# A transformer megakernel on one core: head rows taken in turns from the partitions, a second chunk laid later, MLP weights loaded later

## The chip, the cores and the metric

One core of one Trainium2 chip runs the whole program. The metric is the device time of one execution in microseconds. The kernel before was run three times: 809.21 us is the median, 804.66 the lowest, 817.38 the highest. The execution that was profiled took 811.46 us; its span, from the first to the last instruction on the chip, is 809.7 us.

## What is computed

The input is a (4, 16, 16, 192) image batch, 1,024 tokens of 192 channels, all float32. Three transformer layers follow one another, then a small spectral layer. Each transformer layer is

```
y = layernorm(x);  q, k, v = y @ Wqkv + b            # 12 heads
attn = softmax(q*scale @ k.T + rel_h + rel_w)        # relative positions, decomposed by row and column
x = x + (attn @ v) @ Wproj + b
x = x + gelu(layernorm(x) @ W1 + b1) @ W2 + b2       # 192 -> 768 -> 192
```

Layers 0 and 2 have heads of 16 channels and attend within windows of 14 x 14 tokens (the 16 x 16 image is padded, so there are inner windows, border windows and pad keys). Layer 1 has heads of 48 channels and attends within whole images of 256 tokens. The last part is a Fourier transform of each image, two block-diagonal complex products with a bias, a ReLU and a soft shrink, and the inverse transform.

## The kernel before

Everything stays in SBUF. Five engines run five instruction streams. All of them walk the same list of steps, `all_steps()`, and each engine issues only its own part of a step, so this list alone sets the order on every engine; semaphores (`Count`) connect them. SyncE (SP) issues all DMAs from one queue, in the order of the list, and where it waits, every DMA behind it waits too.

A **chunk** is 96 rows (`CK`) of q and of k: six heads of 16 channels in layers 0 and 2 (two chunks), two heads of 48 in layer 1 (six chunks). For a chunk, TensorE computes q and k (steps `q`, `k`) and the relative terms (`rh`, `rw`) into PSUM, ScalarE copies them out, and they are split into a rounded part and a rest (three planes `QHL`, `KHL`: high, high, low; two planes in layer 1). In layers 0 and 2 VectorE splits q (lines 975 to 991) and GpSimd splits k (lines 765 to 780); in layer 1 GpSimd does both. The buffers `QHL`, `KHL` and `REL` hold one chunk, so a chunk's split may only overwrite them when all heads of the chunk before have been read (`chunk_read`).

The step **`aug`** of a head (lines 641 to 676) gathers its rows by DMA into one slot of the ring `QA`/`KA` (6 slots in layers 0 and 2, 4 in layer 1): `QA<-QHL` (line 656), `KA<-KHL` (line 664), `QA<-REL` (line 674). `QHL` and `KHL` are read from `mine = slice(i * hd, (i + 1) * hd)`, adjacent partitions; `REL` is read from every sixth partition (every second in layer 1). A later head can be gathered only after the `scores` of the head that had its slot.

For each head, TensorE forms the products twice. **`max`**: queries on the partitions, VectorE takes the row maxima (line 1016), splits them (lines 1029, 1033), and **`maxT`** transposes them (line 1184), copies them (line 1040), and writes them by two small DMAs (`QA<-NR`, line 686) as one more row of the head's `QA` slot, "the max row" below. **`scores`**: keys on the partitions, now with the max row, and ScalarE takes the exponential out of PSUM into `PT` (line 880). `max` has two PSUM banks, `scores` three. **`pv`** multiplies by the values for two heads at a time, in five units.

When the heads of a group are done (four in layers 0 and 2, two in layer 1): **`copy_o`** (ScalarE), **`sums`** (`SUMS<-XNOS`), a reciprocal and **`inverse`** (`inverses<-SUMS`, into DRAM), **`divide`** (`OT<-inverses`, 512 KB broadcast back, then GpSimd multiplies, line 792). Then come `proj`, the layer norm and the MLP, whose weights `W1`, `W2` (576 KB each) are loaded at step `scores` 9.0 (head 9, unit 0), lines 687 to 692.

In `windowed_attention` (layers 0 and 2) the list starts with the first chunk and the gathers of heads 0 to 5, then the values. Then stand `q`, `k`, `rh`, `rw` of the second chunk mixed with `max` of heads 0, 1 and 2, and then the main loop: `scores(h, k)` beside `max(h + 3, k)` and two or three `pv` units per head.

Of the kernel before, what the change touches and what calls it, by code (L numbers as in the profile page):

```python
# [32 lines left out]
HEADS, HALF = 12, 6  # L33
# [21 lines left out]
class Layer:  # L55


    def __init__(self, index, head_dim, window, eps, gelu):
# [168 lines left out]
def first_chunk(L, heads):  # L227

    early = [("q", 0, 0)] if L.pads else [("q", 0, 0), ("k", 0, 0)]
    out = [(*unit, 4 + k) for k, unit in enumerate(early)]  # L230
    out.append(("turn", 0, 1, 2))
    out += [(*unit, k % 4) for k, unit in enumerate(u for u in chunk_units(0) if u not in early)]
    out += [("aug", h, 0, 0) for h in range(heads)]
    return out + [("v", t, 0, 4 + 2 * (t % 2)) for t in range(L.vtiles)]


def windowed_attention(L):

    out = first_chunk(L, L.ring)
    units = chunk_units(1)  # L240
# [7 lines left out]
    late = []  # L248
    for h in range(HEADS):
        beside = {k: [] for k in range(L.units)}  # L250
        if h + ahead - 1 < HEADS:
            beside[1].append(("maxT", h + ahead - 1, 0, 0))
        for k, step in late:
            beside[k].append(step)
        late = []
        if h >= 2:
            pair = h // 2 * 2 - 2
            values = [("pv", pair, k, 0) for k in range(L.pv_steps)]
            for k, step in zip((1, 3, 5), values[:3]) if h % 2 == 0 else zip((1, 3), values[3:]):
                beside[k].append(step)  # L260
            if h % 2 and (pair + 2) % L.per_group == 0:
                g = pair // L.per_group
                beside[4] += [("copy_o", g, 0, 0), ("sums", g, 0, 0)]
                late = [(3, ("inverse", g, 0, 0)), (5, ("divide", g, 0, 0))]
        for k in range(L.units):
            out.append(("scores", h, k, 0))
            if k == L.units - 1 and h + L.ring < HEADS:
                out.append(("aug", h + L.ring, 0, 0))
            if h + ahead < HEADS:
                out.append(("max", h + ahead, k, 0))  # L270
            out += beside[k]
    out += [step for _, step in late]
    g = L.groups - 1
    out += [("pv", HEADS - 2, k, 0) for k in range(L.pv_steps)]
    return out + [("copy_o", g, 0, 0), ("sums", g, 0, 0), ("inverse", g, 0, 0), ("divide", g, 0, 0)]


def whole_attention(L):
# [24 lines left out]
    for h in range(0, HEADS, 2):  # L303
# [24 lines left out]
        if (h + 2) % L.per_group == 0:  # L328
            g = h // L.per_group
            out.append(("copy_o", g, 0, 0))  # L330
            out.append(("sums", g, 0, 0))
            finished = [("inverse", g, 0, 0), ("divide", g, 0, 0)]
        else:
            finished = []
    out += finished
    assert not units and not waiting
# [43 lines left out]
def _build(nc, ctx, io, out):  # L380
# [128 lines left out]
    probs_done = count("probs_done", per(lambda L: HEADS * L.units))  # L509
    pv_done = count("pv_done", per(lambda L: HEADS // 2 * L.pv_steps))  # L510
    o_copied = count("o_copied", per(lambda L: 2 * L.groups))
# [86 lines left out]
    def _(sp):  # L598
# [40 lines left out]
        for L, step, h, u, bank in all_steps():  # L639
            n, m = L.index, mem[L.index]  # L640
            if step == "aug":
# [4 lines left out]
                hd, end = L.hd, L.tiles - 1  # L646
                mine = slice(i * hd, (i + 1) * hd)

# [26 lines left out]
            elif step == "maxT":  # L675
# [63 lines left out]
    def _(pool):  # L739
# [23 lines left out]
        for L, step, i, u, bank in all_steps():  # L763
            n, m = L.index, mem[L.index]
            if step == "k" and u == 1 or step == "q" and u == 1 and not L.pads:

# [48 lines left out]
    def _(act):  # L815
        act.wait_ge(*first_in.at(0, 2))
        for L, step, i, u, bank in all_steps():
# [46 lines left out]
            elif step == "scores":  # L864
# [3 lines left out]
                if L.pads:  # L868
                    if h >= 4:
                        act.wait_ge(*pv_done.at(n, L.pv_steps * (h // 2 - 2) + min(k, 4)))  # L870
                    size, at, wide = ((HALF_IN, 2 * k * INNER, 2 * INNER) if k < 4 else
                                      (EDGES, 2 * FIRST_EDGE, 2 * EDGES) if k == 4 else
                                      (L.pc, 2 * FIRST_EDGE + 2 * EDGES, 4 * EDGES))
                    dst, src = m["PT"][0:size, h % 4, at:at + wide], PS[0:size, bank, 0:wide]
                else:
                    if h >= 2:
                        act.wait_ge(*pv_done.at(n, L.pv_steps * (h // 2 - 1) + 2 * (k // 2) + 1))
                    dst, src = m["PT"][:, h % 2, k % 2, (k // 2) * 512:(k // 2 + 1) * 512], PS[:, bank, :]
                act.wait_ge(*scores_psum.at(n, j))
# [37 lines left out]
    def _(dve):  # L917
# [9 lines left out]
        for L, step, i, u, bank in all_steps():  # L927
# [158 lines left out]
    def _(pe):  # L1086
# [12 lines left out]
        for L, step, i, u, bank in all_steps():  # L1099
# [117 lines left out]
            elif step == "pv":  # L1217

                pair = (i, i + 1)
                if i % L.per_group == 0 and u == 0:  # L1220
# [6 lines left out]
                if not L.pads:  # L1227
                    b = u
                    pe.wait_ge(*probs_done.at(n, L.units * (i + 1) + 2 * (u // 2) + 1))
                    for kc in range(2):  # L1230
# [5 lines left out]
                elif u < NB:  # L1236
                    b = u
                    pe.wait_ge(*probs_done.at(n, L.units * (i + 1) + u))
                    for kc in range(2):
# [6 lines left out]
                else:  # L1246
                    pe.wait_ge(*probs_done.at(n, L.units * (i + 1) + L.units - 1))
                    if i == 0:
# [82 lines left out]
def _pack(inputs):  # L1331
# [17 lines left out]
    for L, (prefix, keys) in zip(LAYERS, names):  # L1349
        n = L.index  # L1350
        g1, o1, g2, o2, rh, rw, wp, bp, w1, b1, w2, b2 = (f(prefix + k) for k in keys.split())
        if n == 1:
            wqkv = np.concatenate([f(prefix + k) for k in ("wq", "wk", "wv")], 1)
            bqkv = np.concatenate([f(prefix + k) for k in ("bq", "bk", "bv")])
        else:
            wqkv, bqkv = (f(prefix + k) for k in (("qkv_w", "qkv_b") if n == 0 else ("w_qkv", "b_qkv")))
        col = np.zeros((128, 8 + 2 * L.chunks + FM), np.float32)
        at = 0
# [43 lines left out]
```

## Time and profile before

| | |
|---|---|
| median of 3 runs | 809.21 us |
| profiled execution | 811.46 us, span 809.7 us |
| TensorE busy | 635.9 us (79%) |
| VectorE, ScalarE, GpSimd busy | 252.7, 224.5, 125.7 us |
| chain that ended last: TensorE, DMA, SP's queue | 49%, 17%, 14% |
| packets of SP's DMAs | 56.77 MB, 34.4% of 16 engines' span |

The times in a timeline are counted from the span's start. A number in square brackets behind a row is the engine's idle time just before it, and what ended it. "PEclk" is the TensorE clock that was granted, 1.00 being full (2.4 GHz) and 0.50 the lower level (1.2 GHz). Layer 0 lies at about 0 to 243 us, layer 1 at about 243 to 548, layer 2 at about 548 to 783.

### The profile page before, as it was taken

Reading aid. Unit: us, or ns where it says so; the run is one execution under the profiler, and the core shown is the slowest. Engines: PE = TensorE matmul, PEld = TensorE weight load, DVE = VectorE, ACT = ScalarE, POOL = GpSimd, SP = SyncE. Lnnn points to the kernel's source line nnn. Section 1 sums busy time; section 2 is a strip of 40 time slices with the busy share of each in tenths; the row PEclk is TensorE's granted clock in tenths of the full one; section 3 lists DMA queues with packets and bytes.
Section 4 is the critical chain, followed back from the end, with each engine's and each line's share of the span. In section 5 each row is a group of like instructions: output and inputs, shape, how many; then the busy total and the mean of one; then the engine's idle time right before and its main releaser. Section 6 shows DMA issues by size and latency. Waiting matters only on the chain.

```text
span 809.7 us, 9787 instructions
## 1 busy us (share of the span) xinstructions
PE 635.9 (79%) x3668; PEld 453.1 (56%) x3668; DVE 252.7 (31%) x727; ACT 224.5 (28%) x444; POOL 125.7 (16%) x189
## 2 busy tenths in 40 slices
PE   3916998784999999889696666998358987959997
PEld 1703775463666566557365455665227764636666
DVE  2405766004123424133142003124147760040023
ACT  2200445321332132323232211333004553213220
POOL 2301000112103303222230112203011001131011
PEclk9965699576999969999797688999766995669999
DMA  5790186212204266253527011302911853020001
GB/s 151 151 134 16 19 116 116 54 39 71 54 23 93 58 129 128 58 126 72 118 66 171 29 45 38 107 6 32 141 34 15 112 97 73 25 74 1 0 1 40
DMA packets 24601, 57.41 MB, mean 71 GB/s; under 512 B 7788, under 2 KB 12150, under 8 KB 24458
## 3 DMA queue, kind: packets, MB, share of 16 engines
q1 hardware_dynamic: 24554, 56.77, 34.4%
q8 instruction: 30, 0.49, 0.3%
q14 instruction: 17, 0.14, 0.0%
HBM read 16.93 MB, written 0.93 MB: 22 GB/s over the span
## 4 chain that ended last, share of the span: by engine, by line
PE 49%; DMA 17%; SPq 14%; DVE 8%; issue 6%; POOL 3%; ACT 2%; DVEq 0%; POOLq 0%; ACTq 0%
PE PS L1096 47%; DMA OT<-inverses 7%; SPq L656 4%; DVE NM L1016 3%; DMA QA<-REL 3%; SPq L674 3%; SPq L664 3%; DMA QA<-NR 3%; POOL OT L792 2%; DMA SUMS<-XNOS 2%; PE PS L1108 1%; SPq L686 1%; DMA inverses<-SUMS 1%; DMA PT<-in_qm 1%; SPq L618 1%
## 5 line engine op out<-in xcount | busy, mean ns | idle before, releaser
L1096 PE MATMUL PS<-KA,QA 104*98 104x196 f32 (+3 forms) x432 | 96.5, 326 | 70.1 <-DVE NM L1016 52.6
L1016 DVE TENSOR_REDUCE NM<-PS 98x2 f32<-98x392 f32 (+2 forms) x192 | 103.5, 569 | 84.4 <-PE PS L1096 83.3
L880 ACT ACTIVATE PT<-PS 98x392 f32<-98x392 f32 (+2 forms) x192 | 94.0, 516 | 111.0 <-PE PS L1096 108.7
L1096 PE MATMUL PS<-QA,KA 114*98 114x196 f32 (+2 forms) x480 | 104.6, 336 | 24.8 <-DMA QA<-NR 22.9
L1096 PEld LDWEIGHTS PS<-KA,QA 104*98 104x98 f32 (+3 forms) x432 | 67.1, 200 | 89.1 <-DVE NM L1016 58.3
L1096 PEld LDWEIGHTS PS<-QA,KA 114*98 114x98 f32 (+2 forms) x480 | 79.2, 220 | 51.7 <-DMA QA<-NR 24.6
L1096 PE MATMUL PS<-PT,V 98*32 98x196 f32 (+2 forms) x672 | 89.0, 394 | 1.3 <-ACT XNOS L895 1.3
L792 POOL TENSOR_TENSOR OT<-XNOS,OT 128x512 f32<-128x512 f32 x24 | 29.9, 1268 | 294.0 <-DMA OT<-inverses 294.0
L1096 PE MATMUL PS<-XT,WQKV 96*96 96x512 f32 x128 | 70.1, 687 | 4.7 <-issue 3.8
L1096 PE MATMUL PS<-XT,W 96*128 96x512 f32 x144 | 65.2, 607 | 3.4 <-issue 3.4
L1096 PE MATMUL PS<-WP,OT 128*128 128x192 f32 x192 | 41.1, 383 | 33.2 <-POOL OT L792 33.2
L1096 PEld LDWEIGHTS PS<-WP,OT 128*128 128x128 f32 x192 | 39.1, 230 | 34.8 <-POOL OT L792 27.0
L1096 PEld LDWEIGHTS PS<-PT,V 98*32 98x32 f32 (+2 forms) x672 | 40.4, 133 | 27.3 <-issue 5.2
L1096 PE MATMUL PS<-W,HT 128*128 128x192 f32 x288 | 48.7, 328 | 4.7 <-ACT HT L901 4.7
L1096 PEld LDWEIGHTS PS<-W,HT 128*128 128x128 f32 x288 | 46.6, 190 | 9.6 <-ACT HT L901 9.6
L1096 PEld LDWEIGHTS PS<-XT,W 96*128 96x128 f32 x144 | 27.4, 194 | 35.4 <-issue 34.6
L1003 DVE TENSOR_TENSOR REL<-PS,REL 32x512 fp32r<-32x512 f32 (+5 forms) x64 | 28.7, 479 | 55.6 <-ACT REL L862 55.6
L1046 DVE RECIPROCAL SUMS<-SUMS 128x32 f32<-128x32 f32 (+1 forms) x12 | 3.6, 303 | 129.9 <-DMA SUMS<-XNOS 129.9
L862 ACT ACTIVATE REL<-PS 32x512 fp32r<-32x512 f32 (+5 forms) x64 | 25.0, 429 | 64.2 <-PE PS L1096 62.3
L1096 PEld LDWEIGHTS PS<-XT,WQKV 96*96 96x96 f32 x128 | 22.7, 186 | 32.0 <-issue 31.8
L901 ACT ACTIVATE HT<-PS,COL 128x512 f32<-128x512 f32 x36 | 23.7, 687 | 49.4 <-PE PS L1096 49.4
L1096 PE MATMUL PS<-QD,RB 96*32 96x64 f32 x384 | 36.5, 262 | 0.1
(81 smaller groups left out, 617.9 us busy)
## 6 DMA issues: line engine op xcount, KB each, us to landing
QA<-QHL SPq DMA_DIRECT2D x36, 192.0 KB
OT<-inverses SPq DMA_DIRECT2D x12, 512.0 KB
KA<-KHL SPq DMA_DIRECT2D x24, 228.0 KB
QA<-REL SPq DMA_DIRECT2D x24, 224.0 KB
QA<-QHL SPq DMA_DIRECT2D x12, 384.0 KB
KA<-KHL SPq DMA_DIRECT2D x12, 384.0 KB
KA<-PT SPq DMA_DIRECT2D x12, 313.5 KB
W<-in_w SPq DMA_DIRECT2D x6, 576.0 KB, 7.5
```

The costliest lines, as they stand in the source:

```text
L618: sp.dma_start(raw(m["KA"][L.rel_row:L.rows, 0, s, :]), m["KC"]).then_inc(aug_const.sem, 16)
L656: sp.dma_start(raw(dst), raw(src)).then_inc(aug_in[s].sem, 16)
L664: sp.dma_start(raw(dst), raw(src)).then_inc(aug_in[s].sem, 16)
L674: sp.dma_start(raw(dst), raw(src)).then_inc(aug_in[s].sem, 16)
L686: sp.dma_start(raw(dst), raw(src)).then_inc(max_row_in[p].sem, 16)
L792: nc.gpsimd.tensor_tensor(o, OS[:, k, :], o, ALU.mult).then_inc(o_done.sem, 1)
L862: ins = nc.scalar.activation(dst, src, ACT.Copy)
L880: nc.scalar.activation(dst, src, ACT.Exp).then_inc(probs_done.sem, 1)
L901: nc.scalar.activation(m["HT"][:, i, u * 512:(u + 1) * 512], PS[:, bank, :], L.gelu, bias=COL[n][:, b1:b1 + 1]).then_inc(gelu_done.sem, 1)
L1003: ins = nc.vector.tensor_tensor(lo, src, hi.bitcast(F32), ALU.subtract)
L1016: nc.vector.tensor_reduce(dst, src, AX.X, ALU.max, negate=True).then_inc(max_done.sem, 1)
L1096: return nc.tensor.matmul(dst, lhsT, rhs, start=start, stop=stop, skip_group_check=loose)
```

## The change

There are four edits.

1. **Rows in turns.** The columns of the q and k weights are permuted on the host, so that channel d of head i lies in partition `d * per_chunk + i`. `aug` then reads `slice(i, None, per_chunk)`: 16 partitions six apart in layers 0 and 2, 48 partitions two apart in layer 1. The destination rows are as before.
2. **The order of layers 0 and 2.** The q split gets a step of its own, `split`. Before the first `scores` stand now only `q`, `k` of the second chunk, `max` of heads 0 and 1; `split`, `rh`, `rw` of the second chunk and `max` of head 2 come within the steps of heads 0 and 1. All five `pv` units of a pair stand in the even head behind it, and the maxima are dealt out in proportion to the TensorE columns of the other steps, with a lead of at least 10 units over `scores`.
3. **MLP weights later.** A step `weights` stands behind `scores` 10.1 in layers 0 and 2, and behind all `scores` and `pv` of the last pair in layer 1.
4. `pv_heads` is a name for the pair (2 in every layer; nothing follows from it).

```diff
+        self.pv_heads = 2 if self.pads else 2
...
 def windowed_attention(L):
     out = first_chunk(L, L.ring)
-    ahead = 3
-    for h in range(ahead):
-        out += [(*unit, 2 + k % 2) for k, unit in enumerate(units[2 * h:2 * h + (2 if h < 2 else 4)])]
-        out += [("max", h, k, 0) for k in range(L.max_units)]
-        if h:
-            out.append(("maxT", h - 1, 0, 0))
+    later = chunk_units(1)
+    out += [(*unit, 2 + k % 2) for k, unit in enumerate(later[:4])]
+    ahead = 2
+    out += [("max", 0, k, 0) for k in range(L.max_units)]
+    out += [("max", 1, k, 0) for k in range(2)] + [("maxT", 0, 0, 0)]
+    out += [("max", 1, k, 0) for k in range(2, L.max_units)]
...
+    for h in range(HEADS):
+        first = h - L.pv_heads
+        values = [("pv", first, k, 0) for k in range(L.pv_steps)] if h and h % L.pv_heads == 0 else []
+        for k in range(L.units):
+            main.append((("scores", h, k, 0), 2 * INNER if k < NB else 2 * EDGES if k == NB else 4 * EDGES))
+            if h == 0 and k in (3, 5) or h == 1 and k in (1, 3):
+                if (h, k) == (0, 3):
+                    main.append((("split", 1, 0, 0), 0))
+                main.append(((*later[4 + 2 * h + k // 4 if h == 0 else 6 + k // 2], TR_BANK), 1024))
+            if h == 2 and k == 0:
+                main += [(("aug", m, 0, 0), 0) for m in (L.ring, L.ring + 1)]
+            if h >= 2 and k == L.units - 1 and h + L.ring < HEADS:
+                main.append((("aug", h + L.ring, 0, 0), 0))
+            if k < len(values):
+                main.append((values[k], 8 * INNER if k < NB else 24 * EDGES))
+            main += [(step, 0) for at, step in late if at == k]
...
+        least = step[1] * L.units + step[2] + 10 - ahead * L.max_units if step[0] == "scores" else 0
+        while taken < len(maxima) and (taken * end < spent * len(maxima) or taken < least):
+            out.append(maxima[taken])
+            taken += 1
+            if turned < ahead + (taken - 2) // L.max_units:
+                out.append(("maxT", turned, 0, 0))
+                turned += 1
...
+        if step == ("scores", HEADS - 2, 1, 0):
+            out.append(("weights", 0, 0, 0))
...
-                mine = slice(i * hd, (i + 1) * hd)
+                mine = slice(i, None, L.per_chunk)
...
-            elif step == "scores" and h == HEADS - 3 and u == 0:
+            elif step == "weights":
...
-            elif step == "q" and u == 1 and L.pads:
+            elif step == "split":
...
+        order = np.arange(2 * L.dim).reshape(2 * L.chunks, L.per_chunk, L.hd).transpose(0, 2, 1).ravel()
```

What moves shows at three places. The line numbers of the kernel after are some 22 higher.

VectorE, layer 0, behind the values (`V`). The casts and subtractions of `QHL` are the q split, `NM<-PS` the maxima. Before:

```order
L966 TENSOR_TENSOR V<-PS,VB 120x12x16 x2
L984 CAST QHL<-XNOS 96x784
L984 CAST QHL<-XNOS 96x4x32
L984 CAST QHL<-XNOS 96x4x28
L987 CAST QHL<-QHL 96x1024
L989 TENSOR_TENSOR QHL<-XNOS,QHL 96x784
L989 TENSOR_TENSOR QHL<-XNOS,QHL 96x4x32
L989 TENSOR_TENSOR QHL<-XNOS,QHL 96x4x28
L1016 TENSOR_REDUCE NM<-PS 98x2 x4
L1016 TENSOR_REDUCE NM<-PS 120x1 x2
```

After:

```order
L988 TENSOR_TENSOR V<-PS,VB 120x12x16 x2
L1017 TENSOR_SCALAR OT<-COL 96x192
L1038 TENSOR_REDUCE NM<-PS 98x2 x4
L1038 TENSOR_REDUCE NM<-PS 120x1 x2
...
L1038 TENSOR_REDUCE NM<-PS 98x2 x2
L1062 CAST NR<-PS 20x120
L1006 CAST QHL<-XNOS 96x784
```

The split now stands behind the maxima of heads 0 and 1 and two units of head 2.

TensorE, layer 0, the end of head 1 and the start of head 2 after the change (`IDN,HL` is `maxT` of head 2, `QA,KA` are `scores`, `KA,QA` are `max`, `XNOS,RB` is `rw`):

```order
L1118 MATMUL PS<-XNOS,RB 84x64 x8
L1118 MATMUL PS<-KA,QA 98x196 x2
L1206 MATMUL PS<-IDN,HL 20x120
L1118 MATMUL PS<-QA,KA 120x120 x2
L1118 MATMUL PS<-QA,KA 96x240 x2
L1118 MATMUL PS<-KA,QA 98x196 x2
L1118 MATMUL PS<-QA,KA 98x196 x2
```

Between the transpose and the first `scores` of head 2 (the last row) stand two units of `scores` and one of `max`; before the change, a transpose stood almost two heads ahead of its `scores`.

SP, layer 0, around the first `divide`. `QA<-NR` rows are the max rows, two DMAs each. Before:

```order
L710 DMA OT<-inverses 128x1x1024
L686 DMA QA<-NR 2x8x98
L686 DMA QA<-NR 2x2x120
L686 DMA QA<-NR 2x8x98
L686 DMA QA<-NR 2x2x120
L691 DMA W_0<-in_w_0 96x1536
L692 DMA W_0<-in_w_0 128x1152
```

After:

```order
L732 DMA OT<-inverses 128x1x1024
L708 DMA QA<-NR 2x8x98
L708 DMA QA<-NR 2x2x120
...
L732 DMA OT<-inverses 128x1x1024
L713 DMA W_0<-in_w_0 96x1536
L714 DMA W_0<-in_w_0 128x1152
```

The first max row behind the first `OT<-inverses` was that of head 9 and is now that of head 7; the weights have moved behind the second `OT<-inverses`.

## Rows read from the trace of the kernel before

**Rows 1.** The page: chain by engine, the exponential, the issue of the MLP weights.
```profile
PE 49%; DMA 17%; SPq 14%; DVE 8%; issue 6%; POOL 3%; ACT 2%; DVEq 0%; POOLq 0%; ACTq 0%
...
L880 ACT ACTIVATE PT<-PS 98x392 f32<-98x392 f32 (+2 forms) x192 | 94.0, 516 | 111.0 <-PE PS L1096 108.7
...
W<-in_w SPq DMA_DIRECT2D x6, 576.0 KB, 7.5
```

**Rows 2.** Timeline of TensorE (start us, us, what), layers 0 and 2, `max` of head 0.
```profile
41.59 0.92 PE L1096 MATMUL PS<-KA,QA 104*98 104x196 f32 x4
...
67.52 1.12 PE L1096 MATMUL PS<-KA,QA 104*98 104x196 f32 x4 [25.01 <-DVE NM L1016]
...
596.02 1.12 PE L1096 MATMUL PS<-KA,QA 104*98 104x196 f32 x4 [21.44 <-DVE NM L1016]
```

**Rows 3.** Timeline of VectorE, layer 0, the q split of the second chunk.
```profile
64.17 0.83 DVE L984 CAST QHL<-XNOS 96x784 fp32r<-96x784 f32 x3 [25.05 <-DMA QA<-REL]
```

**Rows 4.** Timeline of SP's queue, layer 0: `QA<-QHL` of heads 1 and 5.
```profile
34.82 2.35 SPq L656 DMA_DIRECT2D QA<-QHL  x1
...
54.96 2.01 SPq L656 DMA_DIRECT2D QA<-QHL  x1
```

**Rows 5.** The chain that ended last, layer 0 (start us, us, what): a gather and a small DMA.
```profile
57.90 5.63 DMA QA<-REL
...
174.83 2.05 DMA SUMS<-XNOS
```

**Rows 6.** Windows of 1 us, layer 0 gathers: busy times, PEclk, DMA share, GB/s.
```profile
38.00:39.00 1.00, 1.00 (x7) 0.73 (x6) 0.60 (x2) 0.00 (x0) 0.00 (x0) 1.00 0.90 258
...
46.00:47.00 1.00, 0.00 (x0) 0.00 (x0) 0.00 (x0) 0.00 (x0) 0.00 (x0) 0.50 0.92 92
...
48.00:49.00 1.00, 0.00 (x0) 0.00 (x0) 0.00 (x0) 0.00 (x0) 0.00 (x0) 0.50 0.90 209
```

**Rows 7.** Timeline of TensorE, layers 0 and 2, from `rh` to `proj`.
```profile
79.12 9.27 PE L1096 MATMUL PS<-XNOS,RB 96*84 96x64 f32 x64
...
92.78 0.66 PE L1096 MATMUL PS<-QA,KA 114*98 114x196 f32 x2
...
107.19 0.27 PE L1184 MATMUL PS<-IDN,HL 120*20 120x120 f32 x1
...
117.86 0.27 PE L1184 MATMUL PS<-IDN,HL 120*20 120x120 f32 x1
...
145.66 0.98 PE L1096 MATMUL PS<-QA,KA 114*98 114x196 f32 x4 [6.15 <-DMA QA<-NR]
...
173.35 5.47 PE L1096 MATMUL PS<-WP,OT 128*128 128x192 f32 x32
...
619.53 0.66 PE L1096 MATMUL PS<-QA,KA 114*98 114x196 f32 x2
...
701.34 5.47 PE L1096 MATMUL PS<-WP,OT 128*128 128x192 f32 x32
```

**Rows 8.** Timeline of SP's queue, layer 0: the first `divide`, two max rows.
```profile
134.28 0.61 SPq L710 DMA_DIRECT2D OT<-inverses  x1
134.93 2.63 SPq L686 DMA_DIRECT2D QA<-NR  x4
```

**Rows 9.** Window behind the pause at 139.51 to 145.66 us, columns as in rows 6.
```profile
146.00:156.00 10.00, 9.37 (x59) 6.39 (x59) 0.27 (x1) 4.58 (x14) 1.80 (x2) 0.50 0.05 15
```

**Rows 10.** Timeline of SP's queue, layer 1: `KA<-KHL` of head 10, `sums` of group 3.
```profile
423.02 1.22 SPq L664 DMA_DIRECT2D KA<-KHL  x2
...
433.67 0.57 SPq L698 DMA_DIRECT2D SUMS<-XNOS  x1
```

**Rows 11.** Timeline of TensorE, layer 1: `max` of head 10.
```profile
430.24 1.22 PE L1096 MATMUL PS<-KA,QA 128*128 128x256 f32 x4 [6.13 <-DMA QA<-REL]
```

**Rows 12.** The chain that ended last, layer 1: `divide` of groups 3 and 4.
```profile
438.76 14.86 DMA OT<-inverses
...
461.07 12.56 DMA OT<-inverses
```

More of the change, by code:

```diff
@@ L231, in first_chunk @@
     out.append(("turn", 0, 1, 2))
-    out += [(*unit, k % 4) for k, unit in enumerate(u for u in chunk_units(0) if u not in early)]
+    for k, unit in enumerate(u for u in chunk_units(0) if u not in early):
+        out.append((*unit, k % 4))
+        if L.pads and unit == ("q", 0, 1):
+            out.append(("split", 0, 0, 0))
     out += [("aug", h, 0, 0) for h in range(heads)]
@@ L239, in windowed_attention @@
     out = first_chunk(L, L.ring)
-    units = chunk_units(1)
-    ahead = 3
-    for h in range(ahead):
-        out += [(*unit, 2 + k % 2) for k, unit in enumerate(units[2 * h:2 * h + (2 if h < 2 else 4)])]
-        out += [("max", h, k, 0) for k in range(L.max_units)]
-        if h:
-            out.append(("maxT", h - 1, 0, 0))
-    late = []
-    for h in range(HEADS):
[L250 to L254, printed above, removed]
-        late = []
[L256 to L271, printed above, removed]
@@ L272, in windowed_attention @@
-    out += [step for _, step in late]
+    later = chunk_units(1)
[4 more added lines that the diff above has]
+    out += [("max", 1, k, 0) for k in range(2, L.max_units)]
+    main, late = [], []
+    for h in range(HEADS):
+        first = h - L.pv_heads
[13 more added lines that the diff above has]
+            main += [(step, 0) for at, step in late if at == k]
+        late = []
+        if values and h % L.per_group == 0:
+            g = h // L.per_group - 1
+            main += [(("copy_o", g, 0, 0), 0), (("sums", g, 0, 0), 0)]
+            late = [(3, ("inverse", g, 0, 0)), (5, ("divide", g, 0, 0))]
@@ new lines, in windowed_attention @@
+    maxima = [("max", m, k, 0) for m in range(ahead, HEADS) for k in range(L.max_units)]
+    end = sum(wide for step, wide in main[:main.index((("scores", HEADS - 2, 0, 0), 2 * INNER))])
+    spent, taken, turned = 0, 0, 1
+    for step, wide in main:
+        out.append(step)
+        spent += wide
+        least = step[1] * L.units + step[2] + 10 - ahead * L.max_units if step[0] == "scores" else 0
[5 more added lines that the diff above has]
+                turned += 1
+        if taken == len(maxima) and turned < HEADS and step[0] == "scores":
+            out.append(("maxT", turned, 0, 0))
+            turned += 1
+        if step == ("scores", HEADS - 2, 1, 0):
+            out.append(("weights", 0, 0, 0))
@@ L273, in windowed_attention @@
     g = L.groups - 1
-    out += [("pv", HEADS - 2, k, 0) for k in range(L.pv_steps)]
+    out += [("pv", HEADS - L.pv_heads, k, 0) for k in range(L.pv_steps)]
     return out + [("copy_o", g, 0, 0), ("sums", g, 0, 0), ("inverse", g, 0, 0), ("divide", g, 0, 0)]
@@ L334, in whole_attention @@
             finished = []
+        if h == HEADS - 2:
+            out.append(("weights", 0, 0, 0))
     out += finished
@@ L764, in _ @@
             n, m = L.index, mem[L.index]
-            if step == "k" and u == 1 or step == "q" and u == 1 and not L.pads:
+            if step in ("q", "k") and u == 1 and not (L.pads and step == "q"):
                 part, done, hi_done, lo_done = (m["QHL"], q_done, q_hi, q_lo) if step == "q" else \
@@ L1217, in _ @@
             elif step == "pv":
-                pair = (i, i + 1)
+                pair = range(i, i + L.pv_heads)
                 if i % L.per_group == 0 and u == 0:
@@ L1228, in _ @@
                     b = u
-                    pe.wait_ge(*probs_done.at(n, L.units * (i + 1) + 2 * (u // 2) + 1))
+                    pe.wait_ge(*probs_done.at(n, L.units * pair[-1] + 2 * (u // 2) + 1))
                     for kc in range(2):
@@ L1237, in _ @@
                     b = u
-                    pe.wait_ge(*probs_done.at(n, L.units * (i + 1) + u))
+                    pe.wait_ge(*probs_done.at(n, L.units * pair[-1] + u))
                     for kc in range(2):
@@ L1246, in _ @@
                 else:
-                    pe.wait_ge(*probs_done.at(n, L.units * (i + 1) + L.units - 1))
+                    pe.wait_ge(*probs_done.at(n, L.units * pair[-1] + L.units - 1))
                     if i == 0:
```

14 lines of the change are left out of this document (8 added, 6 removed).

## The prediction, made before the result was known

> **What bounds the kernel now.** I read the chain of waits first. TensorE makes up 49% of it, but DMA and SP's queue together 31% [rows 1], so gathers and small DMAs decide at some places. Then I read TensorE's timeline for its pauses and, at each, the queue of the engine that ended it.
>
> The largest pause is the same in layers 0 and 2. TensorE starts `max` of head 0 at 41.59 us and stands still until 67.52, 25.01 us; in layer 2 it is 21.44 us [rows 2]. The rows blame VectorE's maxima, but VectorE was idle for the same 25.05 us, in front of the q split of the second chunk, which waited for a gather [rows 3]. The split may write `QHL` only when heads 0 to 5 are all gathered, at 57.90 + 5.63 = 63.53 us [rows 5], and head 0's maxima, whose data were there at 41.59, stood behind it. The reader is to see a queue blocked at its head, not a slow engine.
>
> The gathers come every (54.96 - 34.82) / 4 = 5.03 us [rows 4]. The rate within that period is uneven: 258 and 209 GB/s in two windows, 92 in another [rows 6]. `QA<-REL`, read from every sixth partition, is 56 x 1024 x 4 B = 229 kB, about 1.0 us at the high rate. `QA<-QHL` and `KA<-KHL`, read from 16 adjacent partitions, are 197 + 233 = 430 kB; they are left with 4.0 us, 107 GB/s, as the low window shows.
>
> In the main loop TensorE is the bound: 117.86 - 107.19 = 10.67 us for two heads without a pause [rows 7]. The loop breaks once, for 6.15 us in front of head 9's `scores` [rows 7]: its max row was issued right behind the first `OT<-inverses` at 134.28 [rows 8] and landed 11.4 us after that issue, with the MLP weights issued behind it in the same queue. The granted clock was 0.50 (1.2 GHz) in the window after that pause, with TensorE 94% busy [rows 9].
>
> **Term 1: the first `scores` of layers 0 and 2 come earlier.** VectorE no longer stands behind the split, so the second chunk's `k` and the 12 units of `max` of heads 0 and 1 follow at once. The same work took 79.12 - 67.52 = 11.6 us before [rows 2, 7], so it is over by 53.2 us. Head 0's max row is issued behind all six gathers on SP, and lands behind them. So the gathers now set the first `scores`.
>
> Price of a gather with the rows in turns: no row shows `QHL` read so. It is at worst unchanged, 5.03 us (dearer I exclude: the same bytes in the same number of rows). At best `QHL` and `KHL` go at the 209 GB/s that a strided source had: 430 / 209 = 2.1, so 3.1 us a head. I take 3.6, near the second, since `REL` is the nearest row in every respect but where it lands. Six heads save 6 x 1.43 = 8.6 us: the last lands at 54.9, the max row, a small DMA of 2.05 us [rows 5], at 57.0. The first `scores` move from 92.78 to 57.0, **-35.8 us**. In layer 2, maxima restart at 596.02 against 67.52, so its last gather landed at about 592.0; now 583.4, `scores` at 585.5 in place of 619.53 [rows 7], **-34.0**.
>
> The Trainium skill (SBUF — State Buffer, Door 1: The DMA port swizzle) says that a DMA's speed hangs on how many of 16 ports its partitions reach, that 16 adjacent ones reach 4 of them, measured at 104 GB/s, and that partitions 0 to 63 reach only 8, at 196 GB/s. The 107 GB/s above agree with the first. The second speaks against part of the change, since the destination rows 0 to 47 stay: by it a head takes 659 / 196 = 3.4 us, an estimate, and this term would be 1.2 us larger.
>
> **Term 2: work that now comes behind the first `scores`.** `rh`, `rw` of the second chunk and `max` of head 2 took TensorE from 79.12 to 92.78, 13.7 us, at the lower clock. They may cost half of that at full clock, or all. I take **+12** a layer (6.8 to 13.7).
>
> **Term 3: max rows come late.** A max row needs the transpose, 0.27, two issues of 2.63 / 4 = 0.66 [rows 8], and a small landing, 2.05: 3.6 us. Head 2's transpose now stands three units ahead of its `scores`, less than 1 us: a pause of 3. Head 4's has five exponentials of 0.516 us between [rows 1], 2.6, and the gather of head 8 in front on SP: a pause of 2.5. Behind the transposes of heads 3 and 5 stand two or more `pv` units; those rows are hidden, even behind a gather. Queued behind TensorE's wait are its own maxima, so VectorE waits too. **+5.5** a layer (0 to 12).
>
> **Term 4: the pause at the first `divide` moves.** The 6.15 us in front of head 9 go. Now head 7's max row stands behind `OT<-inverses`, with less lead, and aug of head 11 is ahead of both, but the weights no longer share the DMA engines. I take a new pause of 5 (0 to 10): **-1**.
>
> **Term 5: odd heads.** All `pv` of a pair stands in the even head. An odd head then has only `scores` and a few maxima for TensorE, and 6 x 0.516 = 3.1 us of exponentials. At most 3.1 us a head are extra, at least none; I take 1 for each of five, **+5**.
>
> **Term 6: the clock.** Before, about 21 us behind the pause ran at 0.50; at full clock they would take 10.8 less. New pauses can take it away again. I take **-5** (-10.8 to +15).
>
> Layer 0: -35.8 + 12 + 5.5 - 1 + 5 - 5 = **-19.3**. Layer 2: **-17.5**.
>
> **Term 7: layer 1.** TensorE waits there for `QA<-REL` of a new chunk, 6.13 us in one case [rows 11]. SP's issue from head 10's `KA<-KHL` to the next `sums` takes 433.67 - 423.02 = 10.65 us [rows 10], paced by the gathers. 48 partitions two apart read at best somewhat faster; the first head of each chunk lay in partitions 0 to 47. Bounds are 0 and a third of the 10.65; I take 1.5 us in each of four repeats, **-6**. The weights went out just ahead of group 3's `OT<-inverses`, which took 14.86 us against 12.56 for group 4's [rows 12]: **-2.3**. Their new place is behind the issue of group 4's; they land in 7.5 us [rows 1], under its 12.56, and before the next `sums`. Without that cover the last `sums` would wait for them. In layers 0 and 2 they go out some 15 us before the last `pv`, under TensorE's work.
>
> **At nothing:** `pv_heads` is 2 as before; the permuted weights are the same bytes; the k split on GpSimd waits for the same gathers, and its result is wanted only by head 6's gather, in the steps of head 2.
>
> Sum: -19.3 - 17.5 - 8.3 = -45.1. Against the profiled execution's 811.46 that is 766.4; the median of the runs is 2.25 lower, so I predict **765 us** (rounded up).
>
> **Rivals.**
> - *The source does not matter* (the landing side, or SP's issue, sets the rate). Then the first `scores` come 8.6 us later in each of two layers and layer 1 keeps its 6: 765 + 23 = 788. For it: the destination is unchanged. Against: the uneven rate [rows 6]. 12%.
> - *Nothing comes late.* Terms 3 and 5 are zero and the clock stays full: 10.5 + 5.8 less in each of two layers, 732; half of that, 748. Against: the short lead is in the order itself. 12%.
> - *The clock pays for the pauses, slower than before.* The place is the first `scores` of heads 2, 4 and 7, in both layers. Each wait of a few us for a max row drops the clock to 0.50, as the pause at 145.66 did, and each costs 10.8 us before it returns. With all six, 65 + 2 x 5 (term 6 given back) = 75: 840. It decides from five pauses on, 765 + 10 + 54 = 829. For it: the clock stayed at 0.50 though TensorE was 94% busy [rows 9]. Against: the new pauses are shorter than the 6.15. 4%.
> - *In between.* Two or three such drops, or the row of head 7 late by the whole 11.4 us of the old one: 793 to 820. 12%.
> - *The forecast,* 745 to 788 around 765: 60%.
>
> 2% of 809 us is 16 us, about what can be told from no change: faster means below 793. The forecast, the second rival and most of the first lie there, 0.84; within 2% are the last one and the rest of the first, 0.12; slower, 0.04. The range, 740 to 797, leaves out the lower half of the second rival and most of the in-between.
>
> **What would show it.** Term 1: no pause of over 20 us in `max` of head 0; first `scores` near 57 and 585; `QA<-QHL` issues some 3.6 us apart, and no windows near 92 GB/s. Terms 3 and 4: pauses for `QA<-NR` in front of heads 2, 4 and 7. Term 6: the granted clock in the loop. Term 7: `OT<-inverses` of group 3 near 12.6 us. The prediction fails if the max row of head 0 is held up by more than the six gathers, or if the loop takes much over 96 us from first `scores` to `proj`.

## The result, and the profile after

The change made the kernel slower, by 2%, where I had forecast 765 us: 823.57 us median of 4 runs (819.13 to 826.21) beside 813.3 us of the kernel before on the same chip (804.66 to 818.76). The ratio is 1.0201, 95% interval 1.0104 to 1.0297. The interval leaves open whether it is more than 2%. The profiled execution took 819.13 us (span 817.3) against 811.46. Some executions of a kernel are slower than its others at a lower clock, and ratios leave them out while medians have them in (two of four in e1 and e8, one of four in e2, one of ten in e3, six of ten in e6), so for these kernels the ratio is the number to read.

The page's busy time of TensorE (us, share of the span, instructions) and the chain by engine, to be laid beside 635.9 us (79%) x3668 before and [rows 1]:

```profile
PE 684.0 (84%) x3668; PEld 485.1 (59%) x3668; DVE 258.9 (32%) x727; ACT 224.3 (27%) x444; POOL 126.2 (15%) x189
...
PE 60%; DMA 14%; DVE 7%; issue 6%; SPq 6%; POOL 3%; ACT 3%; DVEq 0%; ACTq 0%; POOLq 0%
```

This is the whole result in one subtraction. TensorE stood idle for 817.3 - 684.0 = 133.3 us, before for 809.7 - 635.9 = 173.8: its pauses are 40.5 us less in sum, as the change aimed at. But the same 3,668 matmuls now take 48.1 us more, 20.0 of them in layer 0 and 24.1 in layer 2 ahead of `proj`. 48.1 - 40.5 = +7.6, the difference of the spans.

SP's queue in layer 0: `QA<-QHL` of heads 1 and 5, which answer to [rows 4], and head 0's max row.

```profile
34.62 0.57 SPq L678 DMA_DIRECT2D QA<-QHL  x1
...
46.84 0.57 SPq L678 DMA_DIRECT2D QA<-QHL  x1
...
50.27 1.78 SPq L708 DMA_DIRECT2D QA<-NR  x2
```

SP issued a gather every (46.84 - 34.62) / 4 = 3.06 us, before every 5.03. The transfers did not keep up. The window over these four periods (length, busy time of PE, PEld, DVE, ACT, POOL, then the granted clock, DMA share, GB/s):

```profile
34.60:46.80 12.20, 11.68 (x46) 6.53 (x44) 3.66 (x10) 3.61 (x6) 0.00 (x0) 1.00 0.97 181
```

The 659 kB of a head are 3.6 us at 181 GB/s. TensorE's timeline, first `scores` of layers 0 and 2, `scores` of heads 2 and 4, the transpose of head 7, and `proj`, beside [rows 7]:

```profile
56.21 0.65 PE L1118 MATMUL PS<-QA,KA 114*98 114x196 f32 x2 [4.17 <-DMA QA<-NR]
...
80.48 0.65 PE L1118 MATMUL PS<-QA,KA 114*98 114x196 f32 x2 [1.61 <-DMA QA<-NR]
...
102.06 0.42 PE L1118 MATMUL PS<-QA,KA 114*98 114x196 f32 x2 [2.28 <-DMA QA<-NR]
...
154.16 0.27 PE L1206 MATMUL PS<-IDN,HL 120*20 120x120 f32 x1 [1.19 <-DVE HL L1055]
...
176.09 4.17 PE L1118 MATMUL PS<-WP,OT 128*128 128x192 f32 x24
...
587.66 0.65 PE L1118 MATMUL PS<-QA,KA 114*98 114x196 f32 x2 [0.96 <-DMA QA<-NR]
...
708.50 3.68 PE L1118 MATMUL PS<-WP,OT 128*128 128x192 f32 x21
```

The first `scores` are 36.6 and 31.9 us earlier than before, and the two `proj` 2.7 and 7.2 us later. From first `scores` to `proj` the loop took 80.6 and 81.8 us before and takes 119.9 and 120.8: 39 us more in each, of which `rh`, `rw` and the maxima of head 2, which now stand behind the first `scores`, explain about the 13.7 that they took before. The rest the windows explain. After, first `scores` to 136 us:

```profile
56.00:136.00 80.00, 68.80 (x389) 51.69 (x391) 34.62 (x95) 22.86 (x57) 5.64 (x3) 0.52 0.26 58
```

Before, the loop until the pause of 6.15 us:

```profile
96.00:138.00 42.00, 40.14 (x372) 29.12 (x371) 29.26 (x91) 23.09 (x55) 0.00 (x0) 1.00 0.71 103
```

The clock was at 0.52, that is nearly always 1.2 GHz, for 80 us, where before it was at 2.4 GHz for 42. TensorE has 389 matmuls in 68.8 busy us, against 372 in 40.1 (not the same mixture: `rh` and `rw` are among the 389). How it got there shows in small windows of the kernel after:

```profile
47.00:48.00 1.00, 0.81 (x2) 0.36 (x2) 0.98 (x3) 0.35 (x1) 0.00 (x0) 1.00 0.91 204
48.00:49.00 1.00, 0.83 (x4) 0.65 (x4) 0.86 (x6) 0.00 (x0) 0.00 (x0) 0.79 1.07 222
49.00:50.00 1.00, 0.90 (x5) 0.44 (x3) 1.00 (x5) 0.00 (x0) 0.00 (x0) 0.50 1.06 163
...
98.00:99.00 1.00, 1.00 (x7) 1.00 (x7) 0.57 (x1) 0.89 (x3) 0.00 (x0) 0.50 1.02 251
99.00:100.00 1.00, 0.78 (x4) 0.54 (x3) 0.18 (x1) 0.96 (x3) 0.00 (x0) 0.61 0.81 151
100.00:101.00 1.00, 0.00 (x0) 0.00 (x0) 0.38 (x1) 0.06 (x1) 0.00 (x0) 1.00 0.75 162
101.00:102.00 1.00, 0.00 (x0) 0.00 (x0) 0.00 (x0) 0.00 (x0) 0.00 (x0) 1.00 0.12 31
102.00:103.00 1.00, 0.94 (x10) 0.62 (x10) 0.00 (x0) 0.42 (x1) 0.00 (x0) 1.00 1.03 289
103.00:104.00 1.00, 1.00 (x8) 0.80 (x4) 0.14 (x1) 0.08 (x1) 0.00 (x0) 0.59 0.97 162
```

The clock falls at 48.6 us, in the maxima of heads 0 and 1, where no pause is above 0.5 us but TensorE is only some 85% busy. It returns at 99.8, just as head 4's max row is late, is up while TensorE stands for 2.28 us, and is gone again 1.1 us after TensorE resumes. It came back for longer at 137 us, after 11 us without a pause, all of them at 0.50:

```profile
126.00:137.00 11.00, 11.00 (x67) 7.18 (x67) 4.13 (x15) 1.36 (x3) 0.00 (x0) 0.50 0.43 110
137.00:152.00 15.00, 13.33 (x119) 9.58 (x118) 10.02 (x28) 6.99 (x20) 2.52 (x2) 0.99 0.01 3
```

### The profile page after: what moved, and what is told of

It is laid out like the page before. It is cut to its first block, busy times and chain, and to the rows that moved or that the text cites. A ratio compares the mean times of both kernels' runs of the same rounds, so it can differ in the third digit from the quotient of the medians.

```text
span 817.3 us, 9787 instructions
## 1 busy us (share of the span) xinstructions
PE 684.0 (84%) x3668; PEld 485.1 (59%) x3668; DVE 258.9 (32%) x727; ACT 224.3 (27%) x444; POOL 126.2 (15%) x189
## 4 chain that ended last, share of the span: by engine, by line
PE 60%; DMA 14%; DVE 7%; issue 6%; SPq 6%; POOL 3%; ACT 3%; DVEq 0%; ACTq 0%; POOLq 0%
PE PS L1118 58%; DMA OT<-inverses 7%; DMA QA<-NR 2%; DMA SUMS<-XNOS 2%; DVE NM L1038 2%; SPq L696 2%; PE PS L1130 2%; POOL OT L814 2%; SPq L686 2%; DMA QA<-REL 1%; DMA inverses<-SUMS 1%; DVE REL L1025 1%; ACT REL L884 1%; SPq L708 1%; SPq L678 1%
## 5 line engine op out<-in xcount | busy, mean ns | idle before, releaser
L1038 DVE TENSOR_REDUCE NM<-PS 98x2 f32<-98x392 f32 (+2 forms) x192 | 106.9, 571 | 142.6 <-PE PS L1118 140.7
L1118 PE MATMUL PS<-QA,KA 114*98 114x196 f32 (+2 forms) x480 | 110.3, 361 | 27.0 <-DMA QA<-NR 20.8
L1118 PE MATMUL PS<-KA,QA 104*98 104x196 f32 (+3 forms) x432 | 111.7, 367 | 20.4 <-DMA QA<-REL 11.8
L1118 PEld LDWEIGHTS PS<-QA,KA 114*98 114x98 f32 (+2 forms) x480 | 88.6, 245 | 44.8 <-DMA QA<-NR 23.2
L1118 PEld LDWEIGHTS PS<-KA,QA 104*98 104x98 f32 (+3 forms) x432 | 78.1, 232 | 56.9 <-issue 28.8
L1118 PE MATMUL PS<-PT,V 98*32 98x196 f32 (+2 forms) x672 | 107.5, 461 | 0.0
L1118 PE MATMUL PS<-XT,W 96*128 96x512 f32 x144 | 68.4, 631 | 3.4 <-issue 3.4
L1118 PE MATMUL PS<-XT,WQKV 96*96 96x512 f32 x128 | 67.4, 664 | 4.6 <-issue 3.6
L1118 PEld LDWEIGHTS PS<-PT,V 98*32 98x32 f32 (+2 forms) x672 | 45.9, 152 | 31.9 <-issue 10.2
L1118 PEld LDWEIGHTS PS<-WP,OT 128*128 128x128 f32 x192 | 40.1, 235 | 35.3 <-POOL OT L814 28.5
L1118 PE MATMUL PS<-XNOS,RB 96*84 96x64 f32 x256 | 32.2, 303 | 5.9 <-DVE REL L1025 5.3
```

The lines of the kernel that those rows point to most:

```text
L1038: nc.vector.tensor_reduce(dst, src, AX.X, ALU.max, negate=True).then_inc(max_done.sem, 1)
L1118: return nc.tensor.matmul(dst, lhsT, rhs, start=start, stop=stop, skip_group_check=loose)
```

## The experiments

Two theories at first. *Clock*: the new order's short waits hold the clock down. *Pauses*: the waits themselves cost the time. Then which part of the change does it. Each ratio is to the kernel before, in the same job.

### The change taken apart: e1, e2, e3

e1 is the kernel before with `slice(i * hd, (i + 1) * hd)` replaced by the slice of rows in turns, and the host's tables to match. e2 is its complement, the new order alone, with `pv` grouped. e3 moves the weights alone:

```diff
+            if h == HEADS - 2 and k == 1:
+                out.append(("weights", 0, 0, 0))
-            elif step == "scores" and h == HEADS - 3 and u == 0:
+            elif step == "weights":
```

> The kernel before with the rows in turns alone. Theory G (gathers): a gather takes about 3.1 us in place of 5.03, so the pause in front of head 0's maxima shrinks from 25 us by about 10 in layers 0 and 2, layer 1 gains 3 to 6: a ratio of 0.965 to 0.98. Rival: the landing rows or SP's issues set the rate and nothing moves, ratio 0.995 to 1.005.

> The kernel before with the new order of layers 0 and 2 alone: adjacent rows, weights at scores 9.0. Theory C (clock): first scores near 64 and 595 us, and the granted clock stays at 0.50 for most of the loop as in the changed kernel, so it is slower than before by 2 to 5%. Rival D (the changed kernel lost its time to the new place of the weights or to the rows in turns): this one is faster than before by 3% or more.

> The kernel before with the weights later alone. The pause in front of head 9's scores shrinks from 6 us to 1 to 4 in layers 0 and 2. If it becomes too short for the clock to fall, up to 11 us more come back in each: ratio 0.965 to 0.985. Rival: the pause comes from OT<-inverses alone, the weights behind it do nothing: 0.995 to 1.005.

Measured: e1 771.39 us, ratio 0.9446 (0.9381 to 0.9512); e2 855.57, 1.0513 (1.0417 to 1.0608); e3 807.26, 0.9958 (0.9923 to 0.9993). All that the change gains comes from the rows in turns, and the new order alone costs 5%. e1 gained more than its 0.965 to 0.98, e2 lost a little more than its 2 to 5%, and e3 falls to its rival (0.995 to 1.005). The product of the three, 0.989, is 3% under the 1.020 of all together: the parts overlap, since turns and order both shorten the same stall (ahead of the first `scores` TensorE waits 9.81 us in e2 and 4.17 in the changed kernel). In e1, TensorE's pause for head 0's maxima and the start of `proj`:

```profile
58.78 1.12 PE L1096 MATMUL PS<-KA,QA 104*98 104x196 f32 x4 [16.73 <-DVE NM L1016]
...
149.17 3.30 PE L1096 MATMUL PS<-WP,OT 128*128 128x192 f32 x13 [2.58 <-POOL OT L792]
```

The stall of 25.01 is 16.73, first `scores` come at 82.59, and the loop takes 66.6 us against 80.6: the pause of 6.15 before head 9 is gone. In e3, with only the weights moved, a pause of 4.18 stays in that place. So the gathers had held up that max row more than the weights, whose move took off 2.0 us. e2's loop, 60 to 190 us:

```profile
60.00:190.00 130.00, 110.00 (x607) 79.73 (x609) 46.90 (x130) 38.07 (x94) 10.45 (x7) 0.50 0.29 52
```

At 1.2 GHz throughout, 85% busy.

### Another opening and the old loop: e4

From the changed kernel, with turns and weights kept, the maxima of heads 0 and 1 still ahead of the split. But then the split, `rh`, `rw` and head 2's maxima come as one block, and the loop is that of before, its maxima three heads ahead and `pv` spread over both heads of a pair:

```diff
-    ahead = 2
+    ahead = 3
+    out.append(("split", 1, 0, 0))
+    out += [(*unit, 2 + k % 2) for k, unit in enumerate(units[4:])]
+    out += [("max", 2, k, 0) for k in range(L.max_units)] + [("maxT", 1, 0, 0)]
```

> The changed kernel, but with the main loop of before: maxima of heads 0 and 1 in front of the q split as in the change, then split, rh, rw and the maxima of head 2 in front of the first scores, then scores, maxima three heads ahead and pv spread over two heads as before. Theory C (the loop's make-up keeps the clock low): the loop runs at 1.00 within some 5 us of its start, ratio 0.93 to 0.955. Rival P (an early start without the 25-us pause in itself leaves the clock low, whatever the loop): it stays at 0.50 for tens of us here too, ratio 0.98 or more.

Measured: 753.83 us (750.35 to 757.13), ratio 0.9305 (0.9256 to 0.9354), the fastest of all, below e1, and in the range of its first theory (0.93 to 0.955). The page and the loop:

```profile
PE 615.4 (82%) x3668; PEld 445.9 (60%) x3668; DVE 260.8 (35%) x727; ACT 223.8 (30%) x444; POOL 126.4 (17%) x189
```

```profile
77.00:78.00 1.00, 1.00 (x8) 0.75 (x7) 0.97 (x6) 0.68 (x2) 0.00 (x0) 0.67 0.58 180
78.00:79.00 1.00, 1.00 (x9) 0.88 (x8) 1.00 (x4) 0.86 (x2) 0.00 (x0) 1.00 1.13 221
...
80.00:130.00 50.00, 46.66 (x450) 32.90 (x449) 28.04 (x86) 27.43 (x69) 2.50 (x2) 1.00 0.43 99
```

Here too the clock fell, at 50.4 us, and TensorE then waited 4.80 us for `REL`; first `scores` come at 71.67, 15.5 later than in the changed kernel. But in the loop nothing is late: the clock returns at 77.7 and stays for 50 us, and `proj` starts at 141.5 in place of 176.1. TensorE is idle for 747.5 - 615.4 = 132.1 us, the changed kernel for 133.3. So all of the 70 us between them is in busy time at another clock: 684.0 - 615.4 = 68.6. That decides for *clock* over *pauses*, as far as two whole kernels can.

### The clock by itself: e5

The changed kernel with 24 added matmuls of 384 columns in each of layers 0 and 2, at places where TensorE waited or the clock fell. Nobody reads their products; each is two instructions in the trace, so 96:

```diff
+                if L.pads and i and (axis or u):
+                    extra(1 if axis else 3, 6)
...
+                if L.pads and k == 0:
+                    extra({0: 7, 2: 6, 4: 6}.get(h, 0), 6 if h < 2 else TR_BANK)
```

> The changed kernel with work added: 24 more matmuls of 96 rows by 128 columns by 384 in each of layers 0 and 2 (7 in front of the first scores of head 0, 6 each in front of those of heads 2 and 4, 5 between rh and rw), whose products nobody reads. They take TensorE about 8 us a layer at full clock, mostly in its waits. Theory C (the time is lost to the clock): the granted clock is 1.00 in the loop, and in spite of the added work it is faster than the changed kernel: below 800 us. Theory D (waits between the engines cost it, the clock follows them): it is 5 to 25 us slower than the changed kernel, 825 to 850.

Measured: 803.63 us, ratio 0.9895 (0.9819 to 0.9971), 3% under the changed kernel, with more work done. That is 3.6 us over the 800 of the first theory, and over 20 under the range of the second. The added matmuls and the loop's windows:

```profile
L1124 PE MATMUL PS<-XT,IDN 96*128 96x384 f32 x96 | 40.0, 569 | 0.0
```

```profile
56.00:72.00 16.00, 14.87 (x113) 11.73 (x112) 9.47 (x26) 5.94 (x17) 4.35 (x3) 1.00 0.01 3
72.00:104.00 32.00, 29.91 (x222) 20.12 (x220) 14.03 (x42) 9.10 (x22) 0.00 (x0) 0.95 0.39 85
104.00:128.00 24.00, 19.90 (x116) 13.57 (x116) 10.22 (x33) 7.03 (x20) 1.92 (x2) 0.62 0.33 80
```

40.0 us of matmuls went in, where I had reckoned 16, and `proj` came at 165.4 in place of 176.1. The page has TensorE busy for 677.8 us of a span of 800.0. Without the added ones that leaves 637.8 us for the kernel's own 3,668 matmuls, where the changed kernel took 684.0 and the kernel before 635.9: of the 48.1 us, 46.2 are back. Idle time went from 133.3 to 122.2. Filling a pause can at best cost nothing; to gain, the rest must run faster. The clock was 1.00 where it had been 0.50. This is the experiment that shows the cause.

### Which part of the order: e6, e7, e8, e9, e10

Besides its opening, dealt between the `scores` of heads 0 and 1, the new loop differs from e4's in two ways: `pv` is grouped in even heads, and the maxima lead less. e6 spreads `pv` in the changed kernel; e7 groups it in e4:

```diff
-            for k, step in zip((1, 3, 5), values[:3]) if h % 2 == 0 else zip((1, 3), values[3:]):
+            for k, step in enumerate(values) if h % 2 == 0 else ():
```

e8 lengthens the lead in the changed kernel:

```diff
-        least = step[1] * L.units + step[2] + 10 - ahead * L.max_units if step[0] == "scores" else 0
+        least = step[1] * L.units + step[2] + 16 - ahead * L.max_units if step[0] == "scores" else 0
```

> The changed kernel with pv of a pair spread over two heads as before (units 0 to 2 in the even, 3 and 4 in the odd head); all else is as changed. Theory C1 (grouped pv keep the clock low): the clock reaches 1.00 early in the loop, 770 to 790 us. Theory C2 (the short lead of the max rows, or rh and rw within heads 0 and 1, keep it low): 0.50 for most of the loop here too, 810 to 835.

> The kernel of e4_opening with all five units of pv of a pair in the even head, as in the change. Theory C1: the clock falls in the loop, 785 us or more against 754. Theory C2 or D: the long lead of the maxima carries it, clock 1.00, 750 to 762.

> The changed kernel with a lead of at least 16 units of maxima over scores in place of 10, one head more. Theory F3 (short leads: each max row arrives late, the pause drops the clock): pauses for QA<-NR go, the clock is 1.00, below 790 us. Theory C1 (grouped pv): the pauses go but the clock stays at 0.50, 805 to 825.

e9 is e8 with e6's spread; e10 is e4 with `ahead = 2` in place of 3.

> The changed kernel with two edits at once: its scores may be placed only 16 units, not 10, behind the last of their maxima, and pv is spread over both heads of a pair. What then still differs from the kernel of e4 in layers 0 and 2 is the opening: here rh, rw, the split's maxima and those of head 2 are dealt out between the scores of heads 0 and 1, there they stand in one block ahead of the loop. Theory O (this mixed opening starts the loop's stretch at the low clock, and neither lead nor pv matters once it has): granted clock 0.50 until about 100 us, proj of layer 0 near 165 to 170, 785 to 800 us, as e8. Theory S (short lead and grouped pv each bring pauses and e8 kept those of the second): clock 1.00 from about 85 us, proj near 150, 755 to 775 us.

> The kernel of e4 with one number changed: maxima run two heads ahead of the scores as in the changed kernel, not three. The block of rh, rw and the split stands ahead of the loop as in e4. Theory L (the short lead alone brings the pauses for max rows, and these the clock): pauses of 1 to 4 us for max rows in front of heads, windows at 0.50 in the loop, proj of layer 0 past 155, 785 to 810 us. Theory O (the opening's mixture is what holds the clock down): pauses of 1 us or so, clock 1.00 from 80 to 130 us as in e4, 750 to 762 us.

| kernel | median us | ratio (95%) | PE busy | idle | waits for `QA<-NR` |
|---|---|---|---|---|---|
| changed | 823.57 | 1.0201 (1.0104 to 1.0297) | 684.0 | 133.3 | 20.8 |
| e6, `pv` spread | 820.68 | 1.0057 (0.9997 to 1.0116) | 673.0 | 132.9 | 22.5 |
| e8, lead 16 | 794.67 | 0.9704 (0.9579 to 0.9829) | 674.7 | 124.9 | 9.2 |
| e9, both | 784.17 | 0.9666 (0.9573 to 0.9760) | 651.6 | 126.8 | 11.7 |
| e10, e4 two ahead | 780.37 | 0.9656 (0.9549 to 0.9764) | 649.4 | 128.0 | 17.3 |
| e7, e4 `pv` grouped | 766.93 | 0.9441 (0.9364 to 0.9518) | 641.2 | 123.9 | 8.9 |
| e4 | 753.83 | 0.9305 (0.9256 to 0.9354) | 615.4 | 132.1 | 8.1 |

Busy, idle and waits are of the profiled execution, which took 807.65 us for e6, its shortest, and 801.50 for e8, its longest. Idle time spans only 124 to 133 us over all seven; busy time goes from 615 to 684, and the medians with it. The lead is the largest part that was tested: 10 to 16 units gives 5.0% of the time of before (1.0201 to 0.9704), and three heads to two in e4 costs 3.5% (0.9305 to 0.9656). Grouping costs 1.4% in e7; in e6 it is 1.4% by the ratio but 0.4% by the medians, and in e9 beside e8 the intervals overlap.

Against their forecasts: e6 lies in the range of C2. e7 lies between both, 5 us over C2's and 18 under C1's. e8 lies between both too, and half of each came: the pause at head 4 went, but the clock was at 0.50 until 95.6 us. In e9 the sign of O came, 0.50 until 99.6 us, with 784.17 us at the lower end of its 785 to 800 and `proj` at 156.2, earlier than its 165; S, with 755 to 775 and the clock back at 85, did not hold.

What the opening is worth stays open, since no pair of runs differs in it alone. Counted in the lists of steps, 10 units of `scores` stand between a head's transpose and its first `scores` in e4, 7 in e9 and 4 in e10 (from head 2 on); the changed kernel has 2 for head 2, 5 for head 4 and 3 for the odd heads near them. So e9 differs from e4 in three units of lead besides the opening, and its 3.6% (0.9666 to 0.9305) are of both. e9 and e10 take the same time with a longer lead in e9, which, if a lead is worth what e10 beside e4 says, speaks for a cost of the mixed opening, with `rh` and `rw` dealt between the first `scores`. They lose the clock at different places: e9 until 99.6 us, with first `scores` at 55.05, e10 from 108.9 to 156.7, with first `scores` at 67.89; `proj` starts at 156.2 and 157.6.

In e10 the theory of the lead shows its mechanism, though the time is 5 us under its range; its rival is 18 over. TensorE in e10, and the clock around its wait:

```profile
108.07 0.42 PE L1105 MATMUL PS<-QA,KA 114*98 114x196 f32 x2 [2.18 <-DMA QA<-NR]
```

```profile
106.00:108.00 2.00, 0.00 (x0) 0.00 (x0) 0.48 (x4) 0.00 (x0) 0.00 (x0) 1.00 0.33 76
108.00:109.00 1.00, 0.93 (x9) 0.83 (x9) 0.29 (x1) 0.41 (x2) 0.00 (x0) 0.96 0.00 0
109.00:110.00 1.00, 1.00 (x8) 0.56 (x8) 0.92 (x3) 0.47 (x2) 0.00 (x0) 0.50 0.12 12
...
112.00:152.00 40.00, 38.40 (x225) 25.81 (x226) 11.53 (x32) 13.69 (x33) 2.50 (x2) 0.50 0.18 54
```

One wait of 2.18 us, the clock falls 0.9 us behind its end, and 40 us at half speed follow with TensorE 96% busy, 16 of them (120 to 136 us) without any pause.

### Warming e4: e11

e4 with added matmuls in its opening and ahead of the last `proj` unit:

```diff
+                if L.pads and i and axis:
+                    extra(2 if u else 8, 6)
...
+                if t == 0 and u:
+                    extra(24, 0, 192)
```

> The kernel of e4 with added matmuls whose products nobody reads, where TensorE stands or runs at the low clock in its trace: 8 and 2 of 384 columns ahead of the units of rw and 3 each ahead of two units of max of head 2 in layers 0 and 2, and 24 of 320 columns ahead of the last unit of proj in every layer. If the low clock at 50 to 80 us comes from TensorE's pauses there, and filling them returns it earlier, the loop gains up to 8 us in each of two layers: 735 to 750 us. If the added matmuls only take their own time (26 us in all at full clock, partly in pauses): 755 to 780 us. e4 had 753.8.

Measured: 771.33 us, ratio 0.9517 (0.9448 to 0.9586), in the range of the second forecast. The matmuls ahead of `proj` share its bank, so this kernel computes `proj`'s first tile wrongly; all of the work is in the time. The clock did what was wanted:

```profile
64.00:144.00 80.00, 72.90 (x650) 52.49 (x648) 39.61 (x124) 37.16 (x90) 2.50 (x2) 1.00 0.33 80
```

and the kernel became 17.5 us slower. The 208 added matmuls were busy for 66.5 us, not the 26 that I had reckoned. First `scores` moved from 71.67 to 77.94 and `proj` from 141.5 to 146.6, so the opening's warming gave 1.2 us in the loop for 6.3. The long blocks ahead of `proj` were busy for 39.3 us and took 33.0 off the waits for `OT` (45.6 to 12.6). And the kernel's own matmuls gained nothing in sum: 682.9 - 66.5 = 616.4 us, in e4 615.4. Added work pays only where it buys tens of microseconds of clock, as in e5.

## Why the prediction was wrong

Against the 766.4 us of the sum, the profiled execution's 819.13 is 52.7 more. By place: layer 0's `proj` moved by +2.7 where the sum had -19.3, a miss of 22.0. From there to layer 2's first `scores` the kernel gained 34.6 where the sum had 42.3, a miss of 7.7: 5.3 in layer 1, 1.4 in layer 2's opening, 0.9 between. Layer 2's loop grew by 39.0 where it had 16.5, a miss of 22.5. The rest is the tail.

**Term 1 was right.** In layer 0 `scores` at 57.0 were expected and came at 56.21. The 585.5 for layer 2 is another matter: it stands on the clock of the kernel before and leaves out the 27.6 us that my own sum takes off ahead of layer 2. That 587.66 lies near it is luck. Counted from layer 2's first `q` matmuls (544.18 us before, 544.89 after), the first `scores` come 32.6 us earlier, for 34.0. The gather is near the 3.6 us that I took: 3.6 by the window of 181 GB/s, and in e1 the maxima restart 8.74 us earlier, 0.74 of it because the first gather is issued earlier, which leaves 8.0 / 6 = 1.33 us a head off the 5.03. The Trainium skill (SBUF — State Buffer, Door 1: The DMA port swizzle) gives 196 GB/s measured for one megabyte into partitions 0 to 63. The trace is near it, 181 GB/s in this window and 195 from 46.8 to 50 us, though a third of a head's bytes, `REL`, land above partition 47.

**Terms 3 and 5, as waits, were about right.** The pauses before heads 2 and 4 are 1.61 and 2.28 us, 3.9 in place of 5.5. Grouping `pv` costs 13 us in e7, some 6.5 a layer in place of 5, but most of that is clock: e7's busy time is 25.8 us above e4's.

**Term 4 left out the main cause.** No pause of 5 us came at head 7, only 1.19 for its transpose. I put the old pause down to the weights as well as to `OT<-inverses`; e1, with the faster gathers, removes it with the weights left in place; e3 moves the weights and keeps 4.18 of it.

**Term 2 gave too little,** as part of the same error: `rh` and `rw` ran at 1.2 GHz among waits for `REL`, and the clock that I let return behind them did not.

**Term 6 is the step that failed.** I took -5 us a layer for the clock, with +15 as its worst. The measured loops are some 22.5 us over the sum in each layer, while the sizes of the waits were right or too high. TensorE's busy time for the same matmuls grew by 20.0 us in layer 0 and 24.1 in layer 2, and e5, with the clock back, has 46.2 of the 48.1 us back. My error was in [rows 9]: I read 0.50 with TensorE 94% busy as the tail of one pause of 6.15 us, and let the new, shorter pauses cost only about half of that tail. It was a warning that the lower clock does not end when the pause ends.

A rival, the clock that pays for the pauses, came nearest, at 829 to 840; it got 4%, since I held pauses shorter than 6.15 against it. Its mechanism came in part. At head 4 the clock fell behind a pause of 2.28 us, and at head 7, at 154.4 us, behind waits of 1.17 and 1.19. But the first and longest stretch at 0.50 began at 48.6 us, ahead of all its three places and without a pause over 0.5 us. The median landed between it and the rival in between (793 to 820).

**Term 7 came in part.** `OT<-inverses` of group 3 in the chain that ended last, beside [rows 12]:

```profile
438.48 12.52 DMA OT<-inverses
```

12.52 for 14.86, the 2.3 of the sum. But the weights then took it back. I had them go out behind the issue of group 4's `OT<-inverses`; the list has them behind the last `sums`, in front of the last `inverse`. A row of SP's queue, and one of the chain that ended last:

```profile
475.73 0.41 SPq L713 DMA_DIRECT2D W<-in_w  x1
...
477.34 4.44 DMA inverses<-SUMS
```

That `inverses<-SUMS` took 1.40 us before, and 1.40 and 1.39 in e1 and e2, which keep the weights at their old place; in e3, e4 and e10, which move them, it took 4.46, 4.63 and 4.52. And TensorE still waits 11.8 us in three places of layer 1 for `QA<-REL`, 15.3 before: 3.5 of my 6. In all, layer 1 went from 304.5 to 301.5 us (its first `q` to that of layer 2): 3.0 of the 8.3.

What stays open: what work gives the clock back. In e4 it returned 6 us into the loop, in the kernel after at 137 us after 11, and in e9 this window stands at 0.50 with TensorE busy in all of it:

```profile
80.00:96.00 16.00, 16.00 (x92) 10.84 (x92) 6.06 (x19) 4.55 (x10) 0.00 (x0) 0.50 0.59 126
```

And e8 and e9 no longer have the pause at head 4, yet run at 0.50 until 95.6 and 99.6 us; which of their waits in `rh` and `rw` (1.95 us at most) does that was not taken apart.

## What to carry to other kernels

Removing a stall by starting a pipeline with less lead can lose more than the stall was worth: sum TensorE's busy time and its idle time apart, before and after, and if busy time grew for the same instructions, read the granted clock by stage. Give operands that arrive by a small DMA a lead of several units in a loop; here three heads instead of two was worth 27 us. Check where in the queue a moved transfer lands: the weights moved here held up a small DMA that the chain needed, for 3.0 us. And test a change in layout apart from a change in order: the layout alone gave 40 us, and with a cleaner order 57.

## What the runs showed that I had not expected

- The clock fell without any pause over 0.5 us: in the kernel after at 48.6 us and in e4 at 50.4, in a stretch where each unit waits 0.19 to 0.48 us for a maximum. The Trainium skill (TensorE: Matmul & The Clock Gate, A second HAM failure mode: psum-queue depth-cycling) tells of short idles between groups of matmuls that make the clock swing; these traces agree.
- Once low, it can stay low without a pause: 40 us at 0.50 with TensorE 96% busy in e10, 100% from 120 to 136 us.
- The clock can be up during a pause and fall just after it: 1.00 from 100 to 103 us in the kernel after, 0.50 from about 103.2.
- SP's issues were no measure of the gathers: with the rows in turns they came 3.06 us apart while the bytes moved at a pace of 3.6. In the kernel before the two agreed: from 34.8 to 55.0 us, four periods of 5.03, the window has 135 GB/s, 2.7 MB, for 2.6 MB issued. By the issues alone a gather looks faster than it is.
